# A one-core transformer block on Trainium2: attention scores taken from fp32 heads instead of stacked bf16 parts

## What is computed

```python
# token mixer: embedding + positions, one-head attention, layernorm over (256, 192), MLP, layernorm
y = emb[x] + pos_encoding
y = layernorm2d(y + softmax(q @ k.T) @ v @ Wo, ...); y = layernorm2d(y + gelu((y @ W1 + b1) @ W2 + b2), ...)
# attention on the row-normalised state: 12 heads of 16, RMS-normed q and k, added to the state
qkv = x @ qkv_w.T + qkv_b
w = softmax(rms_norm(q) @ rms_norm(k).T / 4);  out = (w @ v) @ proj_w.T + proj_b
# mixture of experts: first slots (groups of 64 tokens, 128 slots), second slots, 32 experts, mixing back
xn = l2norm(x) * sqrt(192) * gamma_in;  logits1 = xg @ phi.T
disp1 = softmax(logits1, over tokens); comb1 = softmax(logits1, over slots)
slots = disp1.T @ xg; yn = l2norm(slots) ...; means of 4 slots ...; experts ...
```

## Time and profile before

| | us |
|---|---|
| median of 3 runs | 657.24 |
| the profiled execution: its own time | 661.21 |
| its span, first to last instruction | 659.3 |
| PE, DVE, ACT, POOL busy | 571.6, 371.5, 276.8, 84.2 |
| weights and gather end, mixer begins | 31.8 |
| attention stage | 132.6 to 342.0 |
| first slots | 342.0 to 407.8 |
| second slots and dispatch | 407.8 to about 500 |
| experts and output | about 500 to 659.3 |

### The profile page before, as it was taken

The page is one execution under the profiler, slowest core; times in us unless marked ns, Lnnn a source line. Parts: engine busy times, 40 slices in busy tenths (PEclk is TensorE's granted clock), DMA queues, the critical chain, the costliest instruction groups (busy, mean ns, idle before and its releaser), DMA issues. The chain is left out here.

```text
span 659.3 us, 12622 instructions
## 1 busy us (share of the span) xinstructions
PE 571.6 (87%) x4677; PEld 469.7 (71%) x4677; DVE 371.5 (56%) x928; ACT 276.8 (42%) x803; POOL 84.2 (13%) x114
## 2 busy tenths in 40 slices
PE   6398796787899989988787879999988999999996
PEld 5287786775666666666475556588877999999995
DVE  2126547648899999987524662546663323332332
ACT  1022522324665676555314762736664222222220
POOL 5593000000000000000007510001000000000000
PEclk9789799889899999979878999999999999999999
DMA  9400000000000000000018000400004999999623
GB/s 317 123 1 2 0 1 0 1 1 0 2 2 1 1 0 0 0 2 1 1 63 333 1 1 16 166 1 1 1 1 177 403 310 299 326 291 321 193 43 108
DMA packets 20076, 57.93 MB, mean 88 GB/s; under 512 B 2803, under 2 KB 9573, under 8 KB 19910
## 3 DMA queue, kind: packets, MB, share of 16 engines
q1 hardware_dynamic: 14006, 48.04, 20.3%
q0 software_dynamic: 1024, 4.34, 3.7%
q10 hardware_dynamic: 4992, 4.82, 2.3%
HBM read 52.47 MB, written 4.33 MB: 86 GB/s over the span
## 5 line engine op out<-in xcount | busy, mean ns | idle before, releaser
L2077 DVE SCALAR_TENSOR_TENSOR ex_act_t<-banks,b_sb,ex_gelu 128x128 f32<-128x128 f32 x128 | 36.0, 344 | 95.3 <-ACT ex_gelu L2057 95.3
L2057 ACT ACTIVATE ex_gelu<-banks,b_sb 128x128 f32<-128x128 f32 x128 | 36.5, 368 | 100.8 <-PE banks L2008 100.8
L2003 PE MATMUL banks<-slots_t,w 128*128 128x128 f32 x512 | 62.5, 275 | 1.1 <-PEq L1693 1.1
L2003 PEld LDWEIGHTS banks<-slots_t,w 128*128 128x128 f32 x512 | 61.2, 192 | 1.4 <-issue 1.3
L1095 DVE TENSOR_REDUCE att_max<-banks 128x4 f32<-128x1024 f32 x48 | 58.6, 1221 | 2.6 <-PE banks L751 1.6
L945 ACT ACTIVATE att_prob<-banks 128x1024 f32<-128x1024 f32 x48 | 49.0, 1022 | 17.6 <-PE banks L774 17.6
L2021 PE MATMUL banks<-w,ex_act_t 128*128 128x192 f32 x256 | 50.2, 339 | 0.2 <-DVE ex_act_t L2077 0.2
L257 PE MATMUL banks<-ident 128*128 128x128 f32 x310 | 42.1, 290 | 3.6 <-PEq L263 3.0
L2021 PEld LDWEIGHTS banks<-w,ex_act_t 128*128 128x128 f32 x256 | 40.7, 189 | 4.2 <-DVE ex_act_t L2077 0.5
L257 PEld LDWEIGHTS banks<-ident 128*128 128x128 f32 x310 | 39.5, 204 | 5.6 <-issue 5.5
L2008 PE MATMUL banks<-slots_t,w 64*128 64x128 f32 x512 | 37.2, 285 | 0.0
(11 more groups left out here) (234 smaller groups left out, 1123.0 us busy)
## 6 DMA issues: line engine op xcount, KB each, us to landing
w<-in_w SPq DMA_DIRECT2D x32, 768.0 KB, 8.0
w<-in_w2e SPq DMA_DIRECT2D x32, 384.0 KB, 8.7
w_slot<-in_w_slot SPq DMA_DIRECT2D x8, 576.0 KB, 3.7
rows_scratch<-ex_rows ACTq DMA_DIRECT2D x28, 96.0 KB, 6.6
yn_all<-rows_scratch POOLq DMA_DIRECT2D x7, 384.0 KB, 7.9
out<-h SPq DMA_DIRECT2D x8, 192.0 KB, 2.4
wq_t<-in_wq_t SPq DMA_DIRECT2D x1, 579.0 KB, 5.0
wk_t<-in_wk_t ACTq DMA_DIRECT2D x1, 579.0 KB, 5.5
```

The source lines that it names most:

```text
L2003: nc.tensor.matmul(bank[:, j * P:(j + 1) * P], g.w1[e][:, first + j * P:first + (j + 1) * P], x[:, 0, :], start=(j == 0), stop=False, skip ...
L2057: nc.scalar.activation(gelu[n % 2][:, j * P:(j + 1) * P], gate_bank(n)[:, j * P:(j + 1) * P], ACT.Gelu_apprx_tanh, bias=g.t["b1"][:, n, HB ...
L2077: nc.vector.scalar_tensor_tensor(out=act_t[n % 2][:, j * P:(j + 1) * P], in0=value_bank(n)[:, j * P:(j + 1) * P], scalar=g.t["b1"][:, n, j ...
```

## The change

Attention no longer splits into bf16. g.qk keeps each head of q and k in fp32 in 32 columns: 16 numbers, then one column that holds the negated row maximum (on the side of q) or 1 (of k), then zeros. A quad is one 128-column fp32 transpose per tile of 128 tokens and side (12 per sequence), so head h of a quad stands in rows 32h to 32h + 15 of g.qk_t. A score is an fp32 product over 16 rows (for the maximum) or 17 (for the exponential, the maximum included). scores_and_maxima issues the scores of one pair of heads and the maxima of another in turns, each of the four heads in another group of 32 rows and another bank. turn_max turns a quad of q again, now with its maxima, and keep_max copies it back. Scale and weight of q and k move from DVE to POOL; the squares' input is copied by ACT (keep_qk). The features' weights come in 128 + 64 rows instead of 96 + 96 + bias: qkv_w has its last row subtracted from all rows by POOL in the mixer, and x has a one in its last column, so that the bias takes that row's place. All eight sequences are written out, without a loop. keep_busy calls are placed anew at the stage's start and end, 18 instead of 9 at the mixer's end.

After a sequence is done, DVE takes its row statistics (out_stats) and ACT the roots (root_out), in the attention stage; POOL makes the token rows of sequences 0 to 3 there (make_tokens). In first_slots these steps are gone; POOL makes the rows of 4 to 7, each ahead of a scale_comb. The loop there has three steps more than sequences instead of four. The loads of positions and layernorm weights go ahead of the others and have a semaphore of their own, for which the mixer's DVE and the end of the first stage wait; the mixer's POOL waits for all.

```diff
 fold_weights, SP
+            for name in MIXER_OPERANDS:
+                sp.dma_start(g.t[name], g.d[name]).then_inc(g.mixer_operands_loaded, 16)
...
-            sp.wait_ge(g.operands_loaded, 16 * N_OPERANDS)
+            sp.wait_ge(g.mixer_operands_loaded, 16 * len(MIXER_OPERANDS))
 token_mixer
+            for c in range(3):
+                nc.gpsimd.tensor_tensor(g.t["qkv_w"][:, c, :], g.t["qkv_w"][:, c, :], g.t["qkv_last"], ALU.subtract
+                                        ).then_inc(tok["zero_summed"], 1)
...
-                    keep_busy(nc, g, 1, 9)
+                    keep_busy(nc, g, 1, 18)
 attention, PE
+            def features(cols, half):
+                for t in range(TPS):
+                    if half:
+                        rows = slice(t * GROUP, (t + 1) * GROUP)
+                        last = nc.tensor.matmul(g.ps[FRONT[t]][:, 0:cols.stop - cols.start], x_t[rows, 1, :],
+                                                g.t["qkv_w"][rows, 1, cols], start=False, stop=True)
+                    else:
+                        last = nc.tensor.matmul(g.ps[FRONT[t]][:, 0:cols.stop - cols.start], x_t[:, 2 * t, :],
+                                                g.t["qkv_w"][:, 2 * t, cols], start=True, stop=False)
+                return last
...
+            def scores_and_maxima(score, best):
+                if score:
...
+                    if u == 0:
+                        pe.wait_ge(S["max_kept"], QUADS * n + q + 1)
+                    if count:
+                        pe.wait_ge(S["exped"], count)
+                if best:
...
+                    if count:
+                        pe.wait_ge(S["maxed"], count)
+                for half in range(TPS):
+                    if best:
+                        for hh in range(2):
+                            row = 32 * (2 * bu + hh)
+                            last_best = nc.tensor.matmul(
+                                g.ps[MAXES[hh]][:, half * SEQ:(half + 1) * SEQ],
+                                g.qk_t[bn_ % 2][row:row + HDIM, bq, 0, half * P:(half + 1) * P],
+                                g.qk_t[bn_ % 2][row:row + HDIM, bq, 1, :], start=True, stop=True)
+                    if score:
+                        for hh in range(2):
+                            row = 32 * (2 * u + hh)
+                            last_score = nc.tensor.matmul(
+                                g.ps[SCORES[hh]][:, half * SEQ:(half + 1) * SEQ],
+                                g.qk_t[n % 2][row:row + HDIM + 1, q, 1, half * P:(half + 1) * P],
+                                g.qk_t[n % 2][row:row + HDIM + 1, q, 0, :], start=True, stop=True)
...
             def turn_max(n, q):
                 count = QUADS * n + q
-                pe.wait_ge(S["max_lo"], count + 1)
-                pe.wait_ge(S["exped"], 2 * count)
+                pe.wait_ge(S["maxed"], 2 * count + 2)
+                if count:
+                    pe.wait_ge(S["exped"], 2 * count)
...
+                scores_and_maxima((n, 1, 0), (n, 2, 1))
+                if fill:
+                    fill_quad(n + 1, 0)
+                    fill_quad(n + 1, 1)
+                if prev:
+                    project(n - 1)
+                warm(n, 3, 0)
+                scores_and_maxima((n, 1, 1), nxt(2))
 first_slots, PE
-            for n in range(BATCH + 4):
-                if 0 <= n - 1 < BATCH:
-                    turn_disp(n - 1)
+            for n in range(BATCH + 3):
                 if n < BATCH:
                     logits(n)
-                if n + 1 < BATCH:
-                    turn(n + 1)
+                if n + 2 < BATCH:
+                    turn(n + 2)
...
+                if n < BATCH:
+                    turn_disp(n)
+            keep_busy(nc, g, 1, 6)
 first_slots, POOL
-            for n in range(BATCH):
-                scale_comb(n)
-                if n + 3 < BATCH:
-                    make_x(n + 3)
+            for n in range(BATCH):
+                if n + NX < BATCH:
+                    make_x(n + NX)
+                scale_comb(n)
```

More of the change, by code:

```diff
@@ L43 @@
 SLOT_BUFS = 3
+NX = 4
 EARLY = 4
@@ new lines, in fill_quad @@
+            def fill_quad(n, quad):
+                if quad == 0:
+                    if n == 0:
+                        pe.wait_ge(S["first_weighted"], 2)
+                    else:
+                        pe.wait_ge(S["weighted"], 2 * n)
+                    pe.wait_ge(S["v_kept"], n + 1)
+                if quad == 1 and n == 0:
+                    pe.wait_ge(S["x_kept"], 2)
+                if quad == 2:
+                    pe.wait_ge(S["fill_kept_s"], 2 * n + 1)
+                for w in range(2):
@@ L863, in finish, with warm @@
[L863 to L875 removed]
+            def warm(n, first, last):
+                if n == 0 and first:
+                    keep_busy(nc, g, OUT[1], first)
+                if n == BATCH - 1 and last:
+                    keep_busy(nc, g, FRONT[0], last)
@@ new lines, in _ @@
+            pe.wait_ge(g.qkv_bias_set, 32)
+            keep_busy(nc, g, 0, 8)
+            turn_x(0)
+            keep_busy(nc, g, 0, 3)
+            make_qk(0)
+            make_qk_rest(0)
+            keep_busy(nc, g, 0, 6)
+            make_v(0)
+            make_v_rest(0)
+            keep_busy(nc, g, 0, 3)
+            turn_x(1)
+            for quad in range(QUADS):
+                fill_quad(0, quad)
+            scores_and_maxima(None, (0, 0, 0))
+            keep_busy(nc, g, OUT[1], 4)
```

900 lines of the change are left out of this document (396 added, 504 removed).

## The result

The changed kernel takes 637.6 us (median of 4 runs, 635.94 to 638.0); against the kernel before, 657.24, the ratio is 0.9674 [0.9646, 0.9702], so 19.6 us less. Forecast were 622, with a range of 606 to 642. The side was right and the size was not: 35 us were forecast, and 637.6 lies outside the 612 to 634 that the forecast gave to its own case.

A forecast was written before the change was run, and what follows sets the result against it. DVE was taken to set the loop's pace, PE close behind. Terms -13.0 - 9.0 - 0.7 - 12.3 = -35.0 took the profiled 661.21 to 626.2; the median being 4.0 lower gave 622 us, range 606 to 642.

The forecast's parts named there:

- A round of 1.1 us: Attention loop: eight fp32 products in four groups of 32 rows, all four overlapping, take 1.1 us; range keeps 1.3.
- The rival in which every change of mode is paid on top: Attention: 0.2 us per mode entry on the path, 10 to 19 us come back, 632 to 641 us; chance 0.15.
- Loop -13.0: Attention loop, first maxima to last scores: PE sets the pace, 159.9 us instead of 172.95, so 13.0 less.
- the second quad's 0.5 us: Loop, second quad: turning back waits for ACT, so six transposes and four instructions of v end 0.5 us late.
- the third's 1.1: Loop, third quad: eight transposes and the projection overfill the opening of 1.36 us, 1.1 us late.
- The rival of fill wholly covered: Loop fill all covered, tails overlapping more, and first slots without the POOL wait: 609 us; chance 0.12.
- Start -9.0: Start of attention: x turned 2.4 us earlier, scaling to first maxima 6.8 shorter, 0.2 back: 9.0 us less.
- End -0.7: End of attention: same steps, partly at the lower clock before, new row statistics and roots about 1.5: 0.7 us less.
- First slots -12.3: First slots: first logits -3.7, seven steps -1.6, fillers -2.8 and dispatch turned earlier about -4.2: 12.3 us less.
- The step of 6.1 us: First slots, steps 1 to 4: 6.1 us each, with POOL's new row set ahead of the division as an added wait.
- 36 fillers of 4.18 become 12: First slots, after the last logits: 36 fillers taking 4.18 us become 12, which gives 2.8 us.
- Elsewhere 0: Other stages: load order gains nothing, POOL's new mixer work is less than its old, fillers stand in a wait; 0 us.

The follow-up runs named there:

- Experiment 5: The changed kernel with every product of a round computed twice, in its own group of rows: 689.34 us, ratio 1.0441 against the kernel before.
- experiment 3: The changed kernel with a round's products not interleaved, four for the maxima first, then four for the scores: 637.27 us, ratio 0.9647 against the kernel before.
- Experiment 4: The changed kernel without fillers in attention's first and last sequence, ends of mixer and attention at the old counts: 661.72 us, ratio 0.9995 against the kernel before.
- experiment 6: The changed kernel with POOL's subtractions after DVE's sums, POOL's weights before its row set, first-slots fillers set anew: 623.76 us, ratio 0.9456 against the kernel before.
- experiment 1: The changed kernel with POOL's three mixer subtractions held back until DVE's four sums are done: 634.28 us, ratio 0.9584 against the kernel before.
- experiment 2: The changed kernel with POOL's weights ahead of its new row set in the first slots: 630.49 us, ratio 0.9532 against the kernel before.

## Why the prediction was right in part

- **A round of 1.1 us**, the price on which it hung: measured 1.08. Experiment 5 shows that each tenth of it is worth 5 us, and experiment 3 that four groups overlap without help of the order. The estimate of 1.15 that the prediction made from the Trainium skill (TensorE: Matmul & The Clock Gate, Part 3) lies 0.07 above the measured value, the 1.1 from rows 0.02 above it; the row on the mix was the better source. The rival in which every change of mode is paid on top is out: it asked for a quad of 6.6 at least (two more entries of 0.2), and one takes 6.29. The drain that the Trainium skill (TensorEngine Tiling (Array Packing), Key Properties) names can't be seen apart; whatever it costs lies inside the 1.08.
- **Loop -13.0**: -14.6, close in part by luck. For the middle the mechanism was right: the second quad's 0.5 us did not come, the third's 1.1 is 0.85, and a quad is 0.09 longer, so 19.75 us a sequence and not 20.2. The ends were mis-sized. The first sequence, put at 19.8, takes 27.2; from the first maxima to the last copy are 163.8 us (147.84 to 311.65) where 159.9 were forecast. The old stretch was cut short as well: to the last copy (333.54) it is 179.2 and not 172.95, and "the last scores" at 327.24 are the last but one. Like for like the loop gained 15.4. The rival of fill wholly covered is out.
- **Start -9.0**: -9.6, by the steps named. **End -0.7**: -1.2.
- **The warm ends** had no term. The forecast reckoned all of the new loop at 2.4 GHz and did not name what keeps it there. Experiment 4 puts 22 us on its 53 filler products (106 of 4803 PE instructions). The forecast's loop came true by the change's fillers, for which it gave no reason.
- **First slots -12.3, the step that failed most**: -2.4 and -2.9. The first logits came 3.3 us earlier where 3.7 were forecast. (a) The step of 6.1 us was made of durations at 2.4 GHz. The added wait was there as described, but the clock falls in these steps to the level of 1.2 GHz, and they take up to 9.2. The seven steps are 45.0 us and not 39.3. Of these 5.7 the clock has 4.8, since they take 40.2 in the execution of experiment 3, which had the same waits and the clock nearly held. With POOL's order turned and fillers in steps 0 and 1 it holds (experiment 6); with the waits it fell in all seven traces, for a time that differs. The old steps were not free of this either: the clock was low from 351 to 355 and from 361 to 365, in steps of 5.81 and 7.69 us where the last two take 5.5. (b) "36 fillers of 4.18 become 12" misread the change: 56 instructions stand in the tail, and it gave 3.2 us and not 7. In experiment 6 the tail is 1.3 us shorter again.
- **Elsewhere 0**: "POOL's new work in the mixer is less than what it did on k_t". Less in amount, but beside DVE's sums the old work was three instructions of 0.29 to 0.44 us and then memsets, and the new work is three subtractions of 1.40 that read two large operands from SBUF. 3.6 us, shown by experiment 1. The other 0 to 2 us of the mixer go with the clock in its passes (low from 85 to 89 in the first profile, not in that of experiment 2) and differ between executions.
- **Reference.** The sum was made against an execution 4.0 us above its median, and the changed kernel's profile lay 1.7 below its own. Of the 15.6 us between 622 and 637.6, 9.9 are terms of the sum (35.0 less the 25.1 by which the spans differ), 5.7 are this.

The gain is there in the loop, where it was expected. What went missing was given back in two other stages, by POOL in both.

## What to carry to other kernels

When a wait is added to the engine that sets the pace, price the wait and then look up what its idle time does to the clock: in this kernel a step with a wait of 1.8 us took 6.3 us with the clock up and 9.2 with it down, and in experiment 4 eight microseconds in which PE was busy 6.41 were followed by 30 us at the low clock. It need not fall in each execution, so look at more than one trace. Count the fillers of a change as parts of it, with a term each: here they were worth 17 to 22 us in the changed kernel and 5 in the one before, about as the time at the low clock that they removed. Fillers that outlast the wait that they fill only delay: ten of them held the means back by 1.5 us. Before giving work to an idle POOL, look at what DVE does at that moment: POOL's 4.7 us beside sums with both operands in SBUF cost DVE 3.6. And when a stretch is compared with a forecast of it, take both from the same event to the same event.

## What the runs showed of the hardware

- Products in different groups of 32 rows don't wait for each other's order: a score eight instructions behind starts 0.03 us after the first maximum (experiment 3). Two groups alone take 1.07 us for four products (147.84 to PE's next instruction at 148.91), four groups 1.08 for eight (194.70 to 195.78).
- A clock once at 1.2 GHz stayed there for 30 and 35 us in rounds of 16 rows, with PE busy 99% of 160 to 184 (experiment 4); in the first slots of the changed kernel it rose again after 14 us (331 to 345), in those of experiment 3 after 3 (340 to 343).
- DVE's sum of 128x384 with both operands in SBUF takes 0.55 us alone and 1.75 to 1.81 beside a POOL subtraction of 128x576, which itself goes from 1.40 to 1.71 (experiment 1 and the changed kernel).
